# Score maxima in four 64x64 tiles of TensorE, in eight bursts per head instead of sixteen

## What is computed

```python
content = einsum('bthd,bshd->bhts', q + u_bias, k)
pos     = _rel_shift(einsum('bthd,phd->bhtp', q + v_bias, p))
attn    = softmax((content + pos) / sqrt(dh))
ctx     = einsum('bhts,bshd->bthd', attn, v)
```

## Time and profile before

| | us |
|---|---|
| median of 3 runs | 1071.98 |
| the profiled execution, its own time | 1072.0 |
| its span (first to last instruction) | 1070.1 |
| PE busy (matmuls) | 850.5 (79%) |
| DVE busy | 723.9 (68%) |
| ACT busy | 460.0 (43%) |
| POOL busy | 397.1 (37%) |

### The profile page before, as it was taken

How to read it: one execution, slowest core, us unless ns; L and a number is a source line. 1 busy time by engine, 2 the same in 40 slices (tenths; PEclk the granted TensorE clock), 3 DMA queues, 4 the chain that set the end, 5 groups by cost and what they waited for, 6 DMA issues and landing times.

```text
span 1070.1 us, 21831 instructions
## 1 busy us (share of the span) xinstructions
PE 850.5 (79%) x8587; PEld 644.0 (60%) x8587; DVE 723.9 (68%) x1573; ACT 460.0 (43%) x773; POOL 397.1 (37%) x446
## 2 busy tenths in 40 slices
PE   2483679999999999987457998999999697057774
PEld 1243468888888888875434655666666377025553
DVE  6772435565555655533577888878788588989994
ACT  3860023333333333334455555656556554222331
POOL 6463001433334334335333334434243207323544
PEclk7696789999999999999669999999999899578998
DMA  6056111333243333453100000000000000000111
GB/s 140 1 159 216 42 39 38 79 75 65 67 94 72 72 65 69 90 153 74 25 1 1 2 2 2 2 2 2 1 2 1 1 1 1 0 0 2 23 26 32
DMA packets 69743, 46.45 MB, mean 43 GB/s; under 512 B 35184, under 2 KB 60984, under 8 KB 68920
## 3 DMA queue, kind: packets, MB, share of 16 engines
q1 hardware_dynamic: 52776, 24.72, 10.2%
q0 software_dynamic: 8032, 19.11, 7.0%
q10 hardware_dynamic: 8832, 1.22, 0.7%
HBM read 30.05 MB, written 12.06 MB: 39 GB/s over the span
## 4 chain that ended last, share of the span: by engine, by line
PE 40%; DVE 27%; DMA 9%; POOL 6%; SPq 6%; ACT 6%; issue 5%; ACTq 0%; POOLq 0%; DVEq 0%
PE PS L1059 7%; PE PS L1174 5%; PE PS L1175 5%; PE PS L1176 5%; PE PS L1079 4%; PE PS L1039 3%; PE PS L1063 3%; PE PS L1040 3%; DMA REG<-inverse_sums 3%; SPq L349 2%; DVE HB L1797 2%; DVE XX L1457 2%; DVE REG L1592 2%; DVE XX L1463 2%; DVE AM L1448 2%
## 5 line engine op out<-in xcount | busy, mean ns | idle before, releaser
L1573 DVE TENSOR_REDUCE MX<-PS 128x2 f32<-128x512 f32 x256 | 171.5, 686 | 165.4 <-PE PS L1040 163.7
L776 ACT ACTIVATE REG<-PS 128x1024 f32<-128x1024 f32 x128 | 131.5, 1027 | 242.1 <-PE PS L1063 239.4
L1059 PE MATMUL PS<-XX,TB 96*128 96x64 f16 x2048 | 160.2, 246 | 7.7 <-DMA XX<-NEG 4.5
L1039 PE MATMUL PS<-TM,YY 128*128 128x256 f16 x512 | 129.6, 285 | 31.7 <-DMA YY<-REG 14.9
L1059 PEld LDWEIGHTS PS<-XX,TB 96*128 96x128 f16 x2048 | 133.6, 120 | 23.2 <-issue 12.8
L613 POOL TENSOR_TENSOR HH<-HB,HH 128x512 f16<-128x512 f32 x64 | 75.8, 1184 | 173.8 <-ACT HH L833 173.8
L1040 PE MATMUL PS<-KM,YY 128*128 128x256 f16 x512 | 126.7, 279 | 0.0
L863 ACT ACTIVATE SG<-PS 128x512 f32<-128x512 f32 x128 | 76.2, 595 | 112.1 <-PE PS L1176 111.8
L1797 DVE SCALAR_TENSOR_TENSOR HB<-PS,SG 128x512 f32<-128x512 f32 x128 | 87.6, 684 | 46.0 <-ACT SG L863 46.0
L1063 PE MATMUL PS<-XX,KC 97*128 97x128 f16 x1024 | 108.0, 229 | 0.0
L1174 PE MATMUL PS<-XH,XX 128*128 128x512 f16 x256 | 98.8, 386 | 10.3 <-DVE HB L1797 10.1
(11 more groups left out here) (235 smaller groups left out, 1653.1 us busy)
## 6 DMA issues: line engine op xcount, KB each, us to landing
REG<-inverse_sums POOLq DMA_DIRECT2D x60, 128.0 KB, 3.1
YY<-queries_content ACTq DMA_DIRECT2D x224, 4.0 KB
KC<-keys_strips SPq DMA_DIRECT2D x16, 192.0 KB
keys_strips<-REG POOLq DMA_DIRECT2D x12, 224.0 KB, 7.8
R<-in_L_attn_x SPq DMA_DIRECT2D x32, 64.0 KB, 2.9
queries_position<-REG POOLq DMA_DIRECT2D x2, 960.0 KB, 12.9
queries_content<-REG POOLq DMA_DIRECT2D x2, 960.0 KB, 16.9
XX<-queries_position SPq DMA_DIRECT2D x60, 32.0 KB
```

The lines of the kernel that those rows point to most:

```text
L776: A(P[jt][:, 1024 * up:1024 * up + 1024].rearrange("p (k x) -> p k x", k=2), ST[u % 2], ACT.Exp).then_inc(exp_done, 1)
L1039: mm(o, yp[:, a], TM[p][:, 31 - a:31 - a + T], start=True, stop=False)
L1059: mm(o_pos[:, a], TB[p][0:96, y0:y0 + 128], xp[0:96, 8 * bank + a], start=(a == 0), stop=False, skip_group_check=True)
L1573: nc.vector.tensor_reduce(MX[h % 2][:, 2 * kk:2 * kk + 2], banks[4 + kk % 2].rearrange("p (a j) -> p a j", a=2), AX_X, ALU.max)\
```

## The change

The pass for the maxima runs on quarters of the array. Row halves r hold eight batches each (YP and YC become half as long and use all 128 partitions; TM is loaded twice, into both halves), column halves c hold 64 queries each. A burst is two rounds (i) of four position and four content matmuls of 64x64, 256 moving columns each; tile (r, c) writes partitions 64c and on of bank 4 + r. So eight bursts of 16 matmuls take the place of sixteen bursts of 4, each burst fills both banks, and VectorE reduces both in one instruction (128x1024 to 128x4). For heads above 0 a burst waits for the reduction of the burst right before it (`max_done, n`); head 0, whose bursts have no scores between them, takes banks 6 and 7 in turn. The bursts stand behind k = 0, 2, 3, 5, 7, 8, 10 and 11. The context parts move to k = 3 and k = 11, each right behind a burst.

The other moves: the eight YP loads of the first half stay with SP (64 pieces instead of 128), the eight of the second half go to ScalarE's queue for head 0 and to GpSimd for all others, where they stand between L553 and the wait for the reciprocal. `shift_row` becomes four DMAs instead of one. The wait for the second NEG half moves from k = 2 to k = 4. The columns of XC and the order of the queries in NQB change so that the DMAs of XC are contiguous. The evacuation of the context stands behind the third reduction, the reciprocal behind the seventh.

```diff
-BANKS = (0, 4, 1, 5, 2, 6, 3, 7)
+BANKS = (0, 4, 2, 6, 1, 5, 3, 7)
+BURSTS = (0, 2, 3, 5, 7, 8, 10, 11)
...
-        YP, YC = ([YY[:, (2 * i + j) * N:(2 * i + j + 1) * N] for j in range(2)] for i in range(2))
+        YP, YC = ([YY[:, (2 * i + j) * N // 2:(2 * i + j + 1) * N // 2] for j in range(2)] for i in range(2))
...
+        def maximum_queries(eng, h, src, half, done):
+
+            for s in range(8):
+                rows = 64 * half + 8 * (7 - s)
+                eng.dma_start(YP[h % 2][rows:rows + 8, :].rearrange("p (n s a) -> p s n a", n=8, s=8)[:, s],
+                              src[:, N // 2 * half:N // 2 * half + N // 2].rearrange("p (n s a) -> p s n a", n=8, s=8)[:, s])\
+                    .then_inc(done[h % 2], 16)
+
+        def maximum_banks(h, g):
+
+            return 6 if h == 0 and g % 2 else 4
...
-                sp.dma_start(TM[p][0:64, 0:287], window).then_inc(y_in[p], 16)
+                for half in range(2):
+                    sp.dma_start(TM[p][64 * half:64 * half + 64, 0:287], window).then_inc(y_in[p], 16)
...
-                    sp.wait_ge(max_mm, 16 * h)
+                    sp.wait_ge(max_mm, 8 * h)
...
-                    maximum_queries(h + 1, qvb_d[DH * h + DH:DH * h + 2 * DH, :])
+                    maximum_queries(sp, h + 1, qvb_d[DH * h + DH:DH * h + 2 * DH, :], 0, y_in)
...
+            maximum_queries(gp, 1, NQB[DH:2 * DH, :], 1, y_second)
...
+            def later_queries(h):
+
+                if h < H:
+                    gp.wait_ge(max_mm, 8 * (h - 1))
+                    gp.wait_ge(qvb_out, 16)
+                    maximum_queries(gp, h, qvb_d[DH * h:DH * h + DH, :], 1, y_second)
...
                 gp.dma_start(RC[h % 2][:, :], den_d[h % 2].rearrange("(p x) -> p x", p=128)).then_inc(den_in, 16)
+                later_queries(h + 3)
...
+            later_queries(2)
             for h in range(H - 1):
...
-                row = XC[n % 2][96:97, :].rearrange("p (m t a) -> p t m a", t=2, a=16)
-                act.dma_start(row[:, half], NEG[half][:, :]).then_inc(neg_in[half], 16)
+                row = XC[n % 2][96:97, :].rearrange("p (r m c t a) -> p r c t m a", r=2, m=64, c=2, t=2)
+                for r in range(2):
+                    for c in range(2):
+                        act.dma_start(row[:, r, c, half], NEG[half][64 * c:64 * c + 64, 8 * r:8 * r + 8]).then_inc(neg_in[half], 16)
...
-            for h in range(2):
-                content_rows(h, NAT[NAT_QU][DH * h:DH * h + DH, :], range(B))
+            content_rows(0, NAT[NAT_QU][0:DH, :], range(B))
+            maximum_queries(act, 0, NQB[0:DH, :], 1, y_in)
+            content_rows(1, NAT[NAT_QU][DH:2 * DH, :], range(10))
             shift_row(0, 0)
+            content_rows(1, NAT[NAT_QU][DH:2 * DH, :], range(10, B))
             shift_row(0, 1)
...
+            def maximum_scores(h, g):
+
+
+                p, n, bank = h % 2, 8 * h + g, maximum_banks(h, g)
+                if g == 0:
+                    pe.wait_ge(y_in[p], Y_FIRST[p] + Y_LOADS * (h // 2))
+                    if h:
+                        pe.wait_ge(y_second[p], Y_SECOND * ((h + 1) // 2))
+                if h:
+                    pe.wait_ge(max_done, n)
+                elif g >= 2:
+                    pe.wait_ge(max_done, g - 1)
...
+                for i in range(2):
+                    tiles = [(slice(64 * r, 64 * r + 64), 16 * c + 2 * g + i, banks[bank + r][64 * c:64 * c + 64, T * i:T * i + T])
+                             for r in range(2) for c in range(2)]
+                    for rows, a, o in tiles:
+                        mm(o, yp[rows, a], TM[p][rows, 31 - a:31 - a + T], start=True, stop=False)
+                    for rows, a, o in tiles:
+                        last = mm(o, yc[rows, a], KM[p][rows, :], start=False, stop=True)
                 last.then_inc(max_mm, 1)
...
-                    pe.wait_ge(neg_in[0], 16 * (h + 1))
-                elif k == 2:
-                    pe.wait_ge(neg_in[1], 16 * (h + 1))
+                    pe.wait_ge(neg_in[0], 64 * (h + 1))
+                elif k == 4:
+                    pe.wait_ge(neg_in[1], 64 * (h + 1))
...
-                    if h + 1 < H and k < 12:
-                        for kk in range(16 * k // 12, 16 * (k + 1) // 12):
-                            maximum_scores(h + 1, kk)
-                    if h and k == 4:
+                    if h + 1 < H and k in BURSTS:
+                        maximum_scores(h + 1, BURSTS.index(k))
+                    if h and k == 3:
                         context_part(h - 1, 1, 0)
                         context_part(h - 1, 1, 1)
-                    if k == 12:
+                    if k == 11:
...
+            def maximum(h, g):
+
+                bank = maximum_banks(h, g)
+                ve.wait_ge(max_mm, 8 * h + g + 1)
+                nc.vector.tensor_reduce(MX[h % 2][:, :].rearrange("p (r a) -> p r a", r=2)[:, :, 2 * g:2 * g + 2],
+                                        PS[:, bank:bank + 2, :].rearrange("p r (i j) -> p r i j", i=2), AX_X, ALU.max)\
                     .then_inc(max_done, 1)
...
+                        if g == 2 and h:
                             evacuate_context(h - 1)
-                        if kk == 14 and h:
+                        if g == 6 and h:
                             inverse_sums(h - 1)
```

More of the change, by code:

```diff
@@ L250, in adaln_program @@
         stored = sem("stored")
+        y_second = [sem(f"y_second{p}") for p in range(2)]
         l_feat, stored_last = sem("l_feat"), sem("stored_last")
@@ L344, in maximum_keys @@
                     .then_inc(y_in[h % 2], 16)
-            def maximum_queries(h, src):
-                for s in range(8):
-                    sp.dma_start(YP[h % 2][8 * (7 - s):8 * (7 - s) + 8, :].rearrange("p (b s a) -> p s b a", b=B, s=8)[:, s],
-                                 src.rearrange("p (b s a) -> p s b a", b=B, s=8)[:, s]).then_inc(y_in[h % 2], 16)
             def first_position_queries(h):
@@ L366, in first_content_queries @@
                         to = 24 * w + 8 * k
-                        sp.dma_start(XC[p][to:to + 8, :].rearrange("p (c w i) -> p w c i", c=4, w=4)[:, w],
-                                     NAT[NAT_QU + part][rows, :].rearrange("p (c w i) -> p w c i", c=4, w=4)[:, w]).then_inc(x_in[p], 16)
+                        sp.dma_start(XC[p][to:to + 8, 1024 * w:1024 * w + 1024],
+                                     NAT[NAT_QU + part][rows, 1024 * w:1024 * w + 1024]).then_inc(x_in[p], 16)
             def score_queries(h):
@@ L377, in score_queries @@
                     sp.dma_start(XP[p][24 * j + 16:24 * j + 24, cols], high[:, cols]).then_inc(x_in[p], 16)
[L378 to L380 removed]
+                both, high = qu_d[h].rearrange("k d x -> (k d) x"), qu_d[h, 0]
                 for w in range(4):
[L382 to L383 removed]
+                    cols = slice(1024 * w, 1024 * w + 1024)
+                    sp.dma_start(XC[p][24 * w:24 * w + 16, cols], both[:, cols]).then_inc(x_in[p], 16)
+                    sp.dma_start(XC[p][24 * w + 16:24 * w + 24, cols], high[:, cols]).then_inc(x_in[p], 16)
             sp.wait_ge(prep_done, 4)
@@ L1025, in _ @@
             pe.wait_ge(v_done, 8)
-            def maximum_scores(h, kk):
-                p, n = h % 2, 16 * h + kk
-                if kk == 0:
-                    pe.wait_ge(y_in[p], Y_LOADS * (h // 2 + 1))
-                if n >= 2:
-                    pe.wait_ge(max_done, n - 1)
+            def maximum_scores(h, g):
[8 more added lines that the diff above has]
+                    pe.wait_ge(max_done, g - 1)
                 yp = YP[p][:, :].rearrange("p (m a) -> p a m", a=32)
                 yc = YC[p][:, :].rearrange("p (m a) -> p a m", a=32)
-                for half in range(2):
-                    a = 2 * kk + half
-                    o = banks[4 + kk % 2][:, T * half:T * half + T]
-                    mm(o, yp[:, a], TM[p][:, 31 - a:31 - a + T], start=True, stop=False)
-                    last = mm(o, yc[:, a], KM[p][:, :], start=False, stop=True)
+                for i in range(2):
[5 more added lines that the diff above has]
+                        last = mm(o, yc[rows, a], KM[p][rows, :], start=False, stop=True)
                 last.then_inc(max_mm, 1)
@@ L1074, in context_part @@
                         pe.wait_ge(ev_done, h)
+                    elif jt == 0:
+                        pe.wait_ge(max_done, 8)
                 p = P[jt].rearrange("p (q b x) -> p b q x", q=8, b=B)
@@ L1082, in context_part @@
                     last.then_inc(pv_mm, 1)
-            for kk in range(16):
-                maximum_scores(0, kk)
+            for g in range(8):
+                maximum_scores(0, g)
             for h in range(H):
@@ L1101, in _ @@
             pe.wait_ge(ld_moe, 64)
[L1102 removed]
+            pe.wait_ge(max_done, 8 * H)
             for c in range(12):
@@ L1117, in _ @@
                 for j in range(4):
```

(22 more changed lines are left out.)

56 lines of the change are left out of this document (25 added, 31 removed).

## The result

The changed kernel takes 1092.88 us (median of 4 runs, 1089.17 to 1097.78) against 1072.09 beside it: ratio 1.0185, 95% interval 1.0154 to 1.0217. It is **slower by some 20 us**, where 1061 was forecast. The profiled execution took 1097.8 us (span 1095.9); it is the longest of the four, two of which took 1089, so what is read from its trace adds up to 5 us more than the medians say. Of its 25.8 us over the one before, 13.5 are there when head 2's first burst starts (170.91 against 157.38), 14.4 come between that and head 15's first burst (307.1 us against 292.7), and the rest of the program gives 2 back.

The account below looks back on a forecast made before the run. The prediction took TensorE to bound the attention stage. From 1072.0 us it took 9.0 for shorter heads, added 1.0 for the start and took 3 for the end: 1061 us, own range 1054 to 1068, stated range 1051 to 1078.

Parts of the forecast that it names:

- a round of four tiles: TensorE's maxima: four 64x64 tiles abreast take 0.109 us, bounds 0.109 and 0.44; 32 rounds a head are 3.5 us.
- a switch: TensorE between bursts and score groups: 14 added switches of 0.095 us, +1.3 us a head.
- wait for the reduction: TensorE idles 0.6 us where a single score group stands between bursts, three times a head: +1.8 us.
- head period: Time per head in the attention stage: 21.65 us against 22.29, -0.64, counted in heads 1 to 14 as -9.0 us.
- the start: First heads' loads: no loss at head 1's first burst, head 2's later, +1.0 us in all; bounds -3 and +13.
- the end: Head 15's wait for the second NEG half falls from 4.5 to 2.5 us; -3 us in all, bounds 0 and -7.
- rivals A and B: Rounds of up to 0.22 us, whole up to 1113: A, row halves take turns (0.11); B, weight loads bound (0.04).
- 0.02 at the start of each burst: TensorE's maxima: 0.02 us extra per burst brings a head's rounds from 3.5 to 3.7 us, against 7.0 before.
- Hidden, by a few tenths: ScalarE's queue: shift_row's four DMAs at 0.48 us delay the exponential by 0.55, still in time for its score group.
- I take 0: GpSimd's chain with eight more issues, 20.8 (22.6) us for a head of 21.65: no cost to the whole.
- rival C: GpSimd's chain becomes the bound: issues of 1.12 us, cycle of 25.3 us, whole 1102 us; chance 0.05.
- Rival D: Eight new issues of ScalarE's queue fall into the start's crowded stretch, up to +12: 1073 us, no change; chance 0.08.

Follow-up runs that it names:

- the pair of runs: Changed kernel with four repairs, second-half YP loads on SyncE's queue (1068.9 us), against the same with these loads left with GpSimd (1078.6 us).
- the run with SyncE's loads: Changed kernel with the second-half YP loads of heads 2 to 15 given back from GpSimd to SyncE's queue: 1082.2 us, ratio 1.0090.
- The early rows: Changed kernel with head 2's sixteen content rows issued behind head 0's first four exponentials instead of its last two: 1083.8 us, ratio 1.0094.
- loads of the start: Changed kernel with head 0's second-half YP loads moved from ScalarE's queue to GpSimd, head 1's put behind GpSimd's residual: 1087.3 us, ratio 1.0156.
- four repairs: Changed kernel with second-half YP loads by SyncE's queue, shift_row in twos, the moves of loads of the start, and head 2's content rows early: 1068.9 us.
- the bursts spread: Changed kernel with bursts behind k = 0, 2, 4 to 14, context parts behind k = 4 and 12, second NEG half at u = 7: 1125.8 us.
- combination 2: combination 1 with all of head 1's small loads and half of head 0's content rows on GpSimd: 1055.4 us, ratio 0.9818.
- combination 1: Changed kernel with the four repairs and, from head 2 on, evenly spaced bursts, one of head h+2 behind k = 14: 1063.9 us, ratio 0.9905.
- the runs that leave the loads with GpSimd: Variants of the changed kernel keeping second-half YP loads on GpSimd: with the other three repairs 1078.6 us, with two bursts of head h+2 in head h 1134.7.

## Why the prediction was wrong

By its own steps, with the profiled executions:

| step | forecast | measured |
|---|---|---|
| a round of four tiles | 0.109 us | 0.11, but the first of a burst 0.22 |
| a switch | 0.095 | 0.09 in, 0.10 out |
| start of a burst | 0.02 | 0.11 |
| wait for the reduction | 3 x 0.6 | 3 x 0.56 |
| shift_row's issues | 0.48, hidden | 0.60, a wait of 0.29 |
| head period | 21.65 | 22.72 |
| GpSimd | 0 | +8.8 (by the pair of runs 9.7) |
| the start | +1.0 | +13.5 |
| the end | -3 | -0.7 |

**Right:** the four tiles go abreast and their weight loads too (rivals A and B fell), the switches, the single buffer's waits, the reduction (1.22 us), 0.56 us an issue on GpSimd, SyncE's queue.

**"0.02 at the start of each burst" failed.** The first round of each burst lasts as long as two. It cost 8 x 0.09 = 0.7 us a head, so the forecast gain of 0.64 was gone by this alone. The context part had shown 24 ns for four tiles of which each has all 128 rows; that was taken for this form too. Nothing here shows why it is 0.11. One thing the trace adds: at 1.2 GHz, where the other rounds take 0.21 us, the first takes 0.25 to 0.28. So it hardly follows the clock, 0.22 at the one level and some 0.27 at the other.

**"Hidden, by a few tenths" failed** by just these tenths: with 0.60 for an issue the exponential ends later than summed, +0.29 us a head.

**"I take 0" for GpSimd failed**, which is rival C at another size: not 1.12 us an issue, but a chain summed too short. The forecast had 3.0 us to the end of L553, 4.5 for the issues and 13.3 from the write to the last store. The changed kernel has, on average over the eleven heads from 204.5 to 464.0 us, 4.3 (the sums come back later), 4.5 and 14.3: 23.1 us, against a period of 22.7. Besides, GpSimd stands still twice for nothing that the profile shows, 2.43 us among the stores before 320.89 and the 2.81 us before 446.36 shown above. The eleven heads take 259.4 us, 9.4 more than eleven periods of TensorE: 5.2 are the two stops, the rest is the slow growth. TensorE pays about that, 1.8 and 7.6 us in the two long periods, and the longer one comes right behind the second stop. The kernel before and the run with SyncE's loads have one such stop each, of 3.22 us (before 436.61 and 451.04), and no long period: there the slack covers it. What the stops are is open.

**The start failed most, +12.5 us.** Two things. ScalarE's queue was costed by its tail price: the 16 rows of head 0 took 32.1 us, 2.0 each, beside eight GpSimd loads more in the crowded stretch (0.95 of the DMA engines' time between 72 and 100 us), and SyncE's queue came 4 us later. Then head 0's loop (head 1's first burst to head 2's) was forecast shorter by 0.4 us and became 9.1 longer: at 1.2 GHz and with its waits it reached u = 6 10.8 us later (159.05 for 148.29), and it is there that head 2's rows are issued. Rival D had named the first, at 12 us; its 0.08 was too small. The early rows show that the wait at its end was avoidable: 9.1 us. Of the 13.5, 4.4 are there at head 1's first burst, 6.4 are the loop's lower clock and its waits, and 2.8 are the longer wait at its end (9.9 for 7.1).

**The end**: in head 15 the wait for NEG is 3.8 us instead of 4.5, not 2.5. The later place of the wait gave no more. With the bursts in the same places other runs have 1.8 us (loads of the start) to 5.8 (four repairs) there, so the place of the wait alone does not set it.

What is left when the four repairs are in: 1068.9 for 1061. The period of 22.43 instead of 21.65 is 0.78 x 14 = 11 us, and head 15's wait 3.3 more than forecast; the better start, which the forecast did not have, takes some of it back.

**Open:** why the clock stays low all through head 0's loop. It rose 22 us after head 1's first burst in the changed kernel and 4 us after it in the kernel before; with the bursts spread, which have no waits, 4 us too. But with head 2's rows early, where the bursts and their waits stand as in the changed kernel, it rose after 7. No run varies this alone.

## What to carry to other kernels

When a change takes work from the bounding engine, sum the period of every chain that closes within it (here GpSimd's sums, normalisation and stores), with its DMA latencies from several heads and not from the best one, and keep a few us over: a chain 0.4 us too long, with two stops of 2.4 and 2.8 us, shows nowhere for eight heads and then costs 9 us. A consumer that becomes faster moves its bound to the place where its operands are issued, so the order of its bursts, of the loads and of the shift belong into one sum. And a gain of 3% per head can be invisible under a start that nobody had counted: move the loads of the first heads to the queue with the cheap issue, and issue each head's rows as early as their buffer is free.

## What the runs showed of the hardware

- Four 64x64 tiles (two row halves, two column halves) run abreast: 0.11 us a round of 256 columns, as long as one full matmul. The four weight loads of a round are recorded at 182 to 190 ns each and overlap. The Trainium skill's rule (TensorEngine Tiling (Array Packing), Restrictions, with TensorE: Matmul & The Clock Gate, section LDWEIGHTS) gives, read as four loads in turn, an estimate of 213 ns a round; the trace does not agree. It is about what the first round of a burst takes (0.22 us at 2.4 GHz, 0.25 to 0.28 at 1.2), but no run here separates that.
- In the crowded stretch an issue from ScalarE's queue costs 2.0 to 2.4 us, one from GpSimd 0.52 to 0.56, as in the quiet loop. In combination 2 eight content rows took 4.13 us from GpSimd and eight more 18.98 from ScalarE's queue. Moving issues there made head 0's maxima start 7.6 us earlier (loads of the start), but in the kernel before they started 8 us later. The Trainium skill (DMA: Bandwidth & Descriptors, Rules for kernel authors) says that spreading DMAs over queues gives no bandwidth and saves issue time only; the runs agree with the last part: moving 32 issues brought the first context part 4.8 us forward (combination 2 against 1).
- A wait inside the loop can cost more than itself, as TensorE comes back at 1.2 GHz, eight matmuls in 1.03 us instead of 0.62: so after the 4.07 us of the changed kernel, after 3.05 with the bursts spread, and once after 1.67 in combination 1.
- GpSimd has stops of 2.4 to 3.2 us between two DMA issues or before one for which the profile names nothing. The kernel before has one in the loop, the changed kernel two; the runs that leave the loads with GpSimd have two as well.
